# Dense rows of an audio tower: four experts side by side in 512 columns, one of four results picked by a share, and the ending's calls in another sequence

## The reference

```
# 1 token warp: 750 tokens -> 375
h = gelu(x @ W1 + b1); h = gelu(h @ W2 + b2); lens = sigmoid(h @ W3 + b3), scaled to sum 375
h = interp_weights(cumsum(lens)) @ x
# 2 linear attention, 8 heads of 64
h = h + rmsnorm((softmax(q) @ (softmax(k) v^T)) @ w_out + b_out)     # on layernorm(h)
# 3 switch layer, 16 experts of 128x128, on xf = layernorm(h)
logits = xf @ switch_w.T + switch_b; probs = softmax(logits)
route = argmax(probs); pos = rank of the token among those of its expert, in row order
y = expert_w[route] @ xf + expert_b[route]
out = h + where(pos <= capacity, y, xf) * max(probs)
```

## Time and profile before

| | |
|---|---|
| time, median of 3 runs | 390.05 us (390.02 to 390.54) |
| the profiled execution | 390.38 us, of which its span is 388.7 us |
| granted clock of TensorE, mean | 0.995 |
| PE busy | 373.8 us (96%) |
| DVE busy | 333.9 us (86%) |
| ACT busy | 226.1 us (58%) |
| POOL busy | 111.2 us (29%) |

### The profile page before, as it was taken

The page is one execution under the profiler, slowest core; times in us unless marked ns, Lnnn a source line. Parts: engine busy times, 40 slices in busy tenths (PEclk is TensorE's granted clock), DMA queues, the critical chain, the costliest instruction groups (busy, mean ns, idle before and its releaser), DMA issues.

```text
span 388.7 us, 7889 instructions
## 1 busy us (share of the span) xinstructions
PE 373.8 (96%) x2702; PEld 326.4 (84%) x2702; DVE 333.9 (86%) x915; ACT 226.1 (58%) x432; POOL 111.2 (29%) x137
## 2 busy tenths in 40 slices
PE   8999799999999999999999999999899999999993
PEld 8777688898889888888888888888788889998993
DVE  5687869969897999799998989799999984898996
ACT  5643369617981599249943896279824752584300
POOL 6121301031162216221414033414121420206881
PEclk9999999999999999999999999999999999999997
DMA  7767002002000020003000200100000044141116
GB/s 224 193 194 281 3 1 86 2 2 61 27 21 2 6 83 15 9 0 86 8 16 1 86 2 23 48 0 11 13 2 0 3 115 110 53 129 51 44 42 173
DMA packets 16406, 21.58 MB, mean 56 GB/s; under 512 B 4930, under 2 KB 11928, under 8 KB 15934
## 3 DMA queue, kind: packets, MB, share of 16 engines
q1 hardware_dynamic: 12398, 18.30, 16.3%
q0 software_dynamic: 2880, 2.35, 2.5%
q10 hardware_dynamic: 1088, 0.42, 0.4%
HBM read 14.40 MB, written 6.62 MB: 54 GB/s over the span
## 4 chain that ended last, share of the span: by engine, by line
PE 70%; DVE 14%; issue 7%; ACT 5%; POOL 3%; DVEq 0%; POOLq 0%; ACTq 0%
PE psB L1236 9%; PE psB L1238 9%; PE psB L1237 9%; PE psC L1263 6%; PE psC L1181 4%; PE psC L1182 4%; PE psC L1183 4%; PE psC L1374 4%; PE psC L1354 2%; PE psC L1339 2%; PE psC L1329 2%; PE psA L1181 2%; PE psC L1486 1%; PE psA L1183 1%; PE psA L1182 1%
## 5 line engine op out<-in xcount | busy, mean ns | idle before, releaser
L1236 PE MATMUL psB<-W2h,h1l 128*125 128x512 f32 x184 | 74.7, 406 | 0.2 <-DVE h1l L1888 0.2
L1238 PE MATMUL psB<-W2h,h1h 128*125 128x512 f32 x184 | 72.5, 394 | 0.0
L1237 PE MATMUL psB<-W2l,h1h 128*125 128x512 f32 x184 | 72.4, 394 | 0.0
L672 ACT ACTIVATE h2b<-h2b 125x512 f32<-125x512 f32 x48 | 29.8, 627 | 31.4 <-DVE h2b L1899 31.2
L1238 PEld LDWEIGHTS psB<-W2h,h1h 128*125 128x125 f32 x184 | 34.1, 185 | 8.6
L1236 PEld LDWEIGHTS psB<-W2h,h1l 128*125 128x125 f32 x184 | 34.1, 185 | 7.4 <-DVE h1l L1888 0.5
L1237 PEld LDWEIGHTS psB<-W2l,h1h 128*125 128x125 f32 x184 | 34.2, 186 | 7.0
L1899 DVE TENSOR_TENSOR h2b<-psB,b2r 125x512 f32<-125x512 f32 x48 | 32.7, 685 | 4.6 <-PE psB L1238 4.4
L655 ACT ACTIVATE h<-psA,b1c 128x376 f32<-128x376 f32 x60 | 33.2, 580 | 5.4 <-PE psA L1183 4.1
L1906 DVE CUSTOM_DVE_ANT_0 h2b<-h2b,W3r 125x512 f32<-125x512 f32 x48 | 32.3, 684 | 1.5 <-ACT h2b L672 1.4
L518 POOL TENSOR_TENSOR dx<-xt 125x640 f32<-125x640 f32 x8 | 12.9, 1616 | 64.1 <-PE psC L1263 52.7
(11 more groups left out here) (286 smaller groups left out, 963.5 us busy)
## 6 DMA issues: line engine op xcount, KB each, us to landing
xTf<-in_x_t SPq DMA_DIRECT2D x16, 187.5 KB, 2.5
xt<-in_x SPq DMA_DIRECT2D x8, 336.0 KB
slot_x<-eb_parts SPq DMA_DIRECT2D x2, 960.0 KB, 12.6
basef<-in_L_tok_W SPq DMA_DIRECT2D x4, 256.0 KB, 5.2
ewT<-in_expert_t SPq DMA_DIRECT2D x1, 1024.0 KB, 8.4
ewf<-slot_x SPq DMA_DIRECT2D x2, 480.0 KB, 6.2
h2b<-slot_x SPq DMA_DIRECT2D x2, 480.0 KB, 8.3
slot_y<-h SPq DMA_DIRECT2D x4, 240.0 KB, 2.4
```

The costliest lines, as they stand in the source:

```text
L672: nc.scalar.activation(slot, slot, ACT.Gelu).then_inc(c_g2.sem, 1)
L1236: mm(ps, lo, W2h[:, k, :], start=k == 0, stop=False)
L1237: mm(ps, hi, W2l[:, k, :], start=False, stop=False)
L1238: last = mm(ps, hi, W2h[:, k, :], start=False, stop=k == HK - 1)
```

## The change

The dense rows. The sixteen experts become four groups of four. `own_tokens(b, g)` makes a masked copy for each group instead of each expert (eight copies in all instead of 32, so the ring goes), and `dense(b, n)` multiplies the copy of group *g* for token tile *j* (n = 4 j + g) by the group's four experts side by side: 512 columns, one bank for each tile. The bank then holds four candidate results for every token; `own_rows(b, j)` picks one with four multiply-adds, `y[k] * share[k] + sum`, where `share` is `ck` at the token's place in its group and zero at the three others. Each of the four waits for the one before. What `spread_choice` spreads is now the group's code, made ahead in `route` for rows 6 and 7 by two new instructions; the rest of `route` became `route_rest`. The bias is an fp32r product of 64 partitions, high and low halves of `expert_b` (`group_biases`, `group_columns`). `finish_row` stays for rows 0 to 5.

```
-            def dense(b, e):
-
-                pe.wait_ge(s_only[b], e + 2)
-                for j in range(GJ):
-                    last = mm(banks_dense(b)[j][0:TP, 0:C], only[b][e][:, j * TP:(j + 1) * TP], ewT[:, e, :], start=False, stop=e == E - 1)
-                last.then_inc(s_dense[b], 1)
+
+            def dense(b, n):
+
+                j, g = divmod(n, GROUPS)
+                if n == 0:
+                    dense_banks(b)
+                pe.wait_ge(s_only[b], g + 1)
+                w = ewT[:, GROUP * g:GROUP * (g + 1), :].rearrange("p k f -> p (k f)")
+                ps, of = banks_dense(b)[j][0:TP, :], slice(j * TP, (j + 1) * TP)
+                mm(ps, only[b][g][:, of], w, start=g == 0, stop=False)
+                if g == GROUPS - 1:
+                    pe.wait_ge(s_only[b], GROUPS + 1)
+                    pe.wait_ge(s_bias, 2)
+                    mm(ps, ohT[b][:, of], eb_both[:], start=False, stop=True).then_inc(s_dense[b], 1)
...
+            def shares(b):
+
+                r = b - PRIOR
+                after(dve, c_oh, b, 1)
+                vec.tensor_reduce(place[:, r], oh[:].rearrange("p j (g k) -> p j k g", g=GROUPS), AX.X, ALU.add).then_inc(s_place[b], 1)
+                dve.wait_ge(s_place[b], 1)
+                after(dve, c_ck, b, 1)
+                vec.tensor_tensor(share[:, r], place[:, r], ck[:, b * GJ:(b + 1) * GJ].unsqueeze(2).to_broadcast([TP, GJ, GROUP]), ALU.mult).then_inc(s_share[b], 1)
+
+            def own_rows(b, j):
+
+                dve.wait_ge(s_dense[b], j + 1)
...
+                for k in range(GROUP):
+                    if k:
+                        dve.wait_ge(s_mix[b], j * (GROUP - 1) + k)
+                    done = s_mix[b] if k < GROUP - 1 else s_res if j == GJ - 1 else s_mixed
+                    vec.scalar_tensor_tensor(yg[b][:, j, :], y[:, k * C:(k + 1) * C], share[:, r, j, k:k + 1], yg[b][:, j, :] if k else base[:, i, :],
+                                             ALU.mult, ALU.add).then_inc(done, 1)
...
+                if ends(b):
+                    r = b - PRIOR
+                    vec.tensor_tensor(grp[:, r], eq[:], grank[:].rearrange("p g k -> p (g k)").unsqueeze(1).to_broadcast([TP, GJ, E]), ALU.mult).then_inc(s_grp[b], 1)
+                    dve.wait_ge(s_grp[b], 1)
+                    vec.tensor_reduce(gcode[:, r], grp[:, r], AX.X, ALU.max).then_inc(s_grp[b], 1)
...
+                vec.tensor_copy(eb_both[:], ebs[:]).then_inc(s_bias, 1)
+                dve.wait_ge(s_bias, 1)
+                vec.tensor_tensor(eb_both[32:64], ebs[32:64], eb_both[32:64], ALU.subtract).then_inc(s_bias, 1)
...
-            fetch(3, 0, 3)
-            fetch(4, 0, 3)
-            fetch(0, 0, 3)
-            fetch(2, 0, 3)
```

More of the change, by code:

```diff
@@ L217, in audio_tower @@
         yg = [t.rearrange("p (j c) -> p j c", j=GJ) for t in homes]
[L219 to L224, removed]
+        only = {PRIOR: [t[:].rearrange("p j c -> p (j c)")[:, i * G:(i + 1) * G] for t in (xt_all, xs_all) for i in range(2)],
+                LAST: [qT[:].rearrange("p j a t -> p (j a t)")[:, i * G:(i + 1) * G] for i in range(GROUPS)]}
+        grp = sb("grp", [TP, 2, GJ, E])
+        gcode = sb("gcode", [TP, 2, GJ])
+        place = sb("place", [TP, 2, GJ, GROUP])
+        share = sb("share", [TP, 2, GJ, GROUP])
+        gcol = sb("gcol", [2 * 32, 1])
+        grank = sb("grank", [TP, GROUPS, GROUP])
         rmw = osq
-        ohT = {PRIOR: neg_g[:], LAST: kT[0:TP, 0, 0:G]}
+        ohT = {PRIOR: Wqh[0:2 * 32, 0:G], LAST: Wqh[0:2 * 32, G:2 * G]}
         s_w2h = sem("s_w2h"); s_w2l = sem("s_w2l"); s_h1h = sem("s_h1h"); s_h1l = sem("s_h1l")
@@ L1150, in _ @@
             key_exp(7, 6, 2)
+            take_outputs(2)
+            take_outputs(3)
+            take_v(7, 6, 0)
+            query_exp(7, 2)
+            take_outputs(4)
+            route_exp(6, 5)
+            take_tokens(6)
             take_tokens(7)
+            key_exp(7, 6, 3)
+            take_v(7, 6, 1)
+            take_v(7, 6, 2)
             take_outputs(6)
[L1153 to L1156, removed]
             take_kt(7, 6, 0)
@@ L1728, in _ @@
             layer1(7, 6, 0, 1)
+            layer1(7, 6, 0, 2)
+            layer1(7, 6, 0, 3)
             k_transposed(5, 4, 0)
@@ L1741, in _ @@
             q_transposed(5, 4, 2)
+            layer1(7, 6, 1, 2)
             fold(5, 4, 6)
@@ L1750, in _ @@
             values(6, 5, 1)
+            keys(6, 5, 0)
             values(6, 5, 2)
@@ L1785, in _ @@
             queries(7, 6, 1)
+            queries(7, 6, 2)
             expert_tokens(3)
@@ L1788, in _ @@
             expert_tokens(4)
+            xf_transposed(6, None)
             expert_products(3)
+            keys(7, 6, 0)
             expert_tokens(5)
-            expert_products(4)
-            expert_tokens(6)
-            queries(7, 6, 2)
-            keys(7, 6, 0)
-            xf_transposed(6, None)
-            expert_tokens(7)
             keys(7, 6, 1)
@@ L1800, in _ @@
             logits(6, None)
+            values(7, 6, 0)
+            values(7, 6, 1)
+            values(7, 6, 2)
+            expert_products(4)
+            expert_tokens(6)
             expert_products(5)
+            expert_tokens(7)
             expert_products(6)
             expert_products(7)
-            values(7, 6, 0)
-            values(7, 6, 1)
-            positions(6, None)
             k_transposed(7, 6, 0)
@@ L1809, in _ @@
             k_transposed(7, 6, 2)
-            values(7, 6, 2)
+            positions(6, None)
             q_transposed(7, 6, 0)
+            context(7, 6)
             q_transposed(7, 6, 1)
-            context(7, 6)
+            q_transposed(7, 6, 2)
+            fold(7, 6, None)
             chosen_on_rows(6)
-            fold(7, 6, None)
-            q_transposed(7, 6, 2)
             attend(7, 6)
-            dense_bias(6)
+            dense(6, 8)
+            dense(6, 4)
             dense(6, 0)
@@ L2368, in _ @@
             route(1, 0)
+            route_rest(1, 0)
             key_max(2, 1, 1)
@@ L2637, in _ @@
             finish_row(2)
-            finish_row(7)
+            keep_base(7, 6)
+            shares(7)
+            own_rows(7, 0)
+            own_rows(7, 1)
+            own_rows(7, 2)
             finish_row(3)
@@ L2645 @@
 TJ = 6
-N_CONST = 15
-N_WR = 11
+N_CONST = 16
+N_WR = 12
 N_PREP = 8
```

259 lines of the change are left out of this document (118 added, 141 removed).

## The result

| | before | after |
|---|---|---|
| median of 4 runs, us | 390.30 (390.02 to 390.69) | 392.95 (392.72 to 393.06) |
| ratio, 95% interval | | 1.0065 (1.0052 to 1.0077) |
| span of the profiled run, us | 388.7 | 391.3 |
| granted clock of the dense stretch | 1.00 | 1.00 |

The change makes the kernel 0.65% slower; the forecast was 390.55 and no change to speak of. The time is outside the forecast's range.

The account below looks back on a forecast made before the run. TensorE was to bind: 355.5 + 2.70 + 20.9 + 1.4 + 1.35 + 0.4 = 382.3, plus 1.41, 2.44 and 3.04 gives span 389.2 (VectorE 385.2, gathers 388.5); profiled run 390.9, less 0.33 is 390.55 us, range 388.8 to 392.2.

Parts of the forecast that it names:

- 48 records of 512 columns: TensorE's dense stretch: columns set the pace, 0.437 a record, 20.9 us as before; rival that weight loads do, 8.5 us, chance 0.08.
- six biases: TensorE's dense stretch: bias goes from 12 records (1.3 us) to six fp32r ones (1.4 us), 0.23 each.
- last chain, rows 3 to 5, tail: After TensorE's end at 382.3: last tile's four multiply-adds 1.41, rows 3 to 5 2.44, tail 3.04, giving 389.2.
- the prediction's own rule: Forms that no trace row shows, such as 512-column fp32 records or VectorE's bias instructions, got a lower and an upper bound.
- VectorE end at 385.2: VectorE alone: 349.85 plus 37.8 - 1.3 - 2.8 us of work plus some 1.6 of waits; so not the later engine.
- T + 34.4: GpSimd's gathers: with T the first gather's start, earliest kernel end, from 27.13 + 3.4 + 0.85 + 3.04; 388.5 at T 354.1.
- the rival of the gathers: First gather later than counted, from 354.8 on, so gathers bind; 391.85 us if 4 us late; chance 0.17.
- the dependent steps: VectorE's ending: each multiply-add waiting for the one before costs 0.38 us, a chain of four 1.41, six chains +8.5.
- the delay of T by 2.1: First gather (T) 2.0 us later, at 354.1: ScalarE's third query exponential, counted 5.9 us behind other work, delays `query_sum` and copies.
- the new order closes no waits: Sequence from 262 to 311: TensorE's 1.19 us of waits only change places; same time within 0.3 us.
- The rival that waits close: New order fills waits of 1.19 in the first stretch and 0.78 ahead of `attend`; 1.5 gone, 389.05 us; chance 0.21.
- the Trainium skill's two rules weighed ahead: VectorE semaphores between chained instructions cost nothing extra (chains 6.4 us); TensorE's load-and-matmul spacing is 81 ns at 128 columns, 131 at 512.

Follow-up runs that it names:

- run 1: Changed kernel with the bias product over 128 rows (64 more rows of zeros) instead of 64: 391.21 us, ratio 1.0024 to the kernel before.
- run 3: Changed kernel with the bias in plain fp32 instead of fp32r, still on 64 rows: 395.94 us, one run.
- run 4: Changed kernel with a row's three biases back to back in the middle of its products, fp32r on 64 rows: 391.16 us, ratio 1.0019 to the kernel before.
- run 5: Changed kernel with the bias over 96 rows instead of 64: 391.31 us, one run.
- run 2: Changed kernel with the six bias products of the dense rows left out: 391.10 us, ratio 1.0018 to the kernel before.
- run 8: Run 6 and run 7 together, bias on 128 rows: 390.72 us, ratio 1.0010 to the kernel before.
- run 7: Run 1 with closing multiply-adds interleaved, a semaphore per tile and results leaving in another order: 391.15 us, ratio 1.0020 to the kernel before.
- run 14: Run 12's edits on the changed kernel's own sequence up to `attend`, third query exponential early: 390.67 us, ratio 1.0011 to the kernel before.
- run 6: Run 1 with row 7's third query exponential ahead of three key exponentials and two output copies on ScalarE: 390.93 us, ratio 1.0012 to the kernel before.
- run 9: Run 1 with the calls up to `attend` in the sequence of the kernel before: 391.46 us, ratio 1.0026 to the kernel before.
- run 12: Run 9 with most closing multiply-adds interleaved, and codes, columns, bias instructions and row 0's closing steps moved on VectorE: 389.54 us, ratio 0.9979 to the kernel before.
- run 13: Run 12 with the bias back on 64 rows: 391.05 us, ratio 1.0018 to the kernel before.

## Why the prediction was wrong

| step | predicted | measured in the profiled run |
|---|---|---|
| first gather | 354.1 | 354.20 |
| `attend` of row 7 | 355.5 | 355.50 |
| first dense product, 2.70 on | 358.2 | 358.23 |
| 48 records of 512 columns | 20.9 | 48 x 0.4275 = 20.5 |
| six biases | 1.4 | 3.7 |
| transposes, logits, positions | 1.35 | 1.44 |
| wait for row 7's tokens | 0.4 | 0.51 |
| last dense product ends | 382.3 | 384.4 |
| last chain, rows 3 to 5, tail | 1.41, 2.44, 3.04 | 1.43, 2.44, 2.93 |
| span | 389.2 | 391.3 |

The six biases are what the stretch from 358.23 to 384.4 leaves when the other three rows are taken off.

**The step that failed** is one sentence of the TensorE part: "The bias goes from 12 records (1.3) to six fp32r ones (1.4)." Its 0.23 was the step of an fp32r record between others with as many rows. The new one has 64 rows between products of 128, and that costs 0.39 more at each visit (runs 1, 3, 4 and 5), 2.3 in all. With the 48 records 0.4 shorter and the other products and the wait together 0.2 longer than counted, this makes the 2.1 between 382.3 and 384.4, and between 389.2 and 391.3. No row of before showed such a neighbour at 512 columns, so by the prediction's own rule it had to be bounded from both sides; it was taken as known. A smaller one stood in the trace of before, 16 products of 64 rows (with 64 columns of weights) between taller ones:

```profile
75.08 0.40 PE L1238 MATMUL psB<-W2h,h1h 128*125 128x512 f32 x1
75.41 0.67 PE L1366 MATMUL psC<-wo,cbd 64*64 64x128 f32 x16
76.00 1.25 PE L1263 MATMUL psC<-dx,A 125*125 125x128 f32 x9
```

```profile
75.41 0.43 PEld L1366 LDWEIGHTS psC<-wo,cbd 64*64 64x64 f32 x16 [0.38 <-issue]
```

The step into them is 0.33, where records like the one ahead go 0.23 to 0.24 apart, and their first load too starts only with its own product. By single records the next two steps on the way out are about 0.1 longer each as well, so the visit costs some 0.3: this was the nearest row for the price. The Trainium skill (TensorEngine Tiling (Array Packing), "Key Properties") says that going from one tiling mode to another drains the engine. The price once per run of three (1.07, run 4) and none at 96 rows (run 5) agree with it, but no trace shows whether a product of 64 rows runs in another mode. This speaks against the change and should have been weighed.

**A second term was too small, but hidden.** The prediction let VectorE end at 385.2, so that TensorE was the later one. With the bias gone VectorE still ends at 386.4 (run 2). Its work fell at least as far as forecast: from the last output copy on it is busy for 32.38 us in run 2 (7.12 of 8.59 up to the first dense product, 25.26 of 28.42 behind it), and the gaps of 0.04 between 18 dependent steps add 0.7, against 33.7 counted. What was wrong is the waits: 3.9 where 1.6 was counted. (In the earlier trace rows VectorE is idle 1.30 ahead of 358.01 and 0.82 behind it, 2.1 in all, so 1.6 was already less than what before showed.) Part of the work removed stood ahead of `m`, where VectorE waits for TensorE's context anyway (1.01 in the changed kernel); behind it stand the waits of 0.38 and 0.64 of run 2, two of 0.27 and 0.36 for ScalarE, and gaps too short to be listed. That is why a cheap bias alone gives 391.2, 0.24% over the kernel before, and not the forecast.

**The gathers' constant** was T + 34.4; the runs in which row 5 waits give 35.1 (run 8), 35.3 (run 7) and 35.4 (run 14, slowest execution: 389.5 - 354.06). The sum took the median landing of the earlier trace rows, 3.4, where the last gather's counts; the longest there is 4.3. So the rival of the gathers, a T later than counted, did not come about (354.20 against 354.1). Small was the constant, and with it the gathers decide from a T of about 353.8 to 354.1, which is the forecast's own T. They were not the cause here, where TensorE ended later still; run 14 shows them bind once TensorE and VectorE are out of the way.

**Right were** the records of 512 columns (the weight loads do not set their pace: 0.4275, not 0.18), the dependent steps (0.38; run 7 shows that the wait, not PSUM, makes them dear), and the delay of T by 2.1 as a number. Its parts do not add up as they are listed: two query exponentials, three key exponentials, four copies and its own come to 4.3, not 5.9. The stretch is 5.85 long in the trace (337.62 to 343.47), and three more copies, to `xfT`, `h` and `v`, stand in it for some 1.3; so the total was luck.

**That the new order closes no waits was wrong**, and luck in the sum. From row 4's `attend` to row 6's the kernel before takes 81.9 us (244.29 to 326.22) and the changed one 81.3 (244.90 to 326.22); the runs with the new sequence all show 81.3 (1, 2, 6, 7, 14), those with the earlier one 81.9 (9, 12, 13). So it closes 0.6 there. In this profile the changed kernel had lost as much ahead of row 4's `attend` (0.3 to 0.8 in those of its edits), and behind row 6's the first gather is 2.1 later. The rival that waits close was right in part.

Of the Trainium skill's two rules weighed ahead, neither held for these forms: a step that waits for the one before it costs 0.12 more than one with another between, and the spacing at 512 columns in fp32 is 0.4275.

## What to carry to other kernels

Price a small product by its neighbours and not by its own size, and look in the trace for a row of that kind, however small: between products of 128 rows, one of 64 cost 0.39 us a visit, which padding with zeros to 96 or 128 rows takes away and putting such products side by side shares out. When a removed cost gives back less than it was worth, look for the next line at once; here three engines' ends lay within a microsecond, and only a version that moved all three was faster than the kernel before. And work that is cut is worth nothing where its engine waits anyway, so subtract it stretch by stretch.

## What was not expected of the hardware

- An fp32r product of 512 columns over 64 rows, alone between fp32 products of 128 rows, takes 0.63 us; over 96 or 128 rows it takes 0.24. In plain fp32 the surcharge is the same 0.39, and three in a row pay it once.
- A multiply-add on VectorE that needs the one before starts 0.38 after it; with one independent instruction between, each step is 0.26, though the semaphore waits are the same.
